# One sequence through all experts at once, the mixer and routing on a new timetable, and ScalarE in the mixer's norm

## The reference

```
x = x + 0.5 * ffn(layernorm(x))        # phase 1
x = x + mixer(layernorm(x))
x = x + 0.5 * ffn(layernorm(x))        # phase 2, same weights

ffn:   logits = tokens @ router_w.T    # 8 experts, top 2, softmax over the two
       each token: sum over its 2 experts of weight * (gelu(t @ w1[e]) @ w2[e])
       # w1[e] is 128x256, w2[e] is 256x128
mixer: v = x @ value_W.T; gates = sigmoid(x @ gate_W.T)   # 9 gates of 128
       out = sum over 9 shifts s of roll(v, -s) * gate_s   # shifts 0, +-1, +-4, +-16, +-32
       return layernorm(out) * gamma + beta
```

## Time and profile before

| | us |
|---|---|
| device time, median of 3 runs | 508.68 |
| lowest and highest of them | 504.05, 509.39 |
| device time of the profiled execution | 505.95 |
| its span, first to last instruction | 504.2 |
| TensorE busy with matmuls | 347.4 (69%) |
| VectorE busy | 286.4 (57%) |
| GpSimd busy | 254.5 (50%) |
| ScalarE busy | 181.6 (36%) |
| mean granted TensorE clock | 0.883 |

### The profile page before, as it was taken

One profiled execution on the slowest core, in us unless ns is written; L12 is line 12 of the kernel. 1 busy time (PEld: TensorE's weight loads), 2 busy tenths in 40 slices (PEclk: granted clock), 3 DMA queues, 4 the chain that ended last, 5 costly groups with the idle time before them and its releaser, 6 DMA issues.

```text
span 504.2 us, 8967 instructions
## 1 busy us (share of the span) xinstructions
PE 347.4 (69%) x2115; PEld 283.8 (56%) x2115; DVE 286.4 (57%) x1076; ACT 181.6 (36%) x422; POOL 254.5 (50%) x264
## 2 busy tenths in 40 slices
PE   1341885688899889996959977499753986288300
PEld 1330885587567756775537764277643975187300
DVE  6558054006666899889993699954997260020011
ACT  1010542343466456552425533355421342044100
POOL 0177717377767204767056173272664747570172
PEclk9999998798999999997779976889985798589955
DMA  8944447558527633453264242543447445845321
GB/s 253 297 142 137 148 136 225 158 157 254 178 88 203 190 106 89 121 157 115 69 183 121 86 150 90 155 111 101 145 150 215 135 142 166 245 128 155 101 73 47
DMA packets 102176, 74.66 MB, mean 148 GB/s; under 512 B 9704, under 2 KB 98032, under 8 KB 102128
## 3 DMA queue, kind: packets, MB, share of 16 engines
q1 hardware_dynamic: 93936, 57.30, 39.3%
q0 software_dynamic: 8192, 16.79, 11.2%
HBM read 48.50 MB, written 25.56 MB: 147 GB/s over the span
## 4 chain that ended last, share of the span: by engine, by line
PE 54%; DVE 15%; issue 12%; POOL 6%; DMA 5%; ACT 4%; SPq 2%; POOLq 0%; ACTq 0%; DVEq 0%
PE ps_u L341 16%; PE ps_u L402 14%; PE ps_d L353 14%; PE ps_t L331 5%; DMA xg<-xs 3%; PE ps_r L373 3%; DVE x_res L658 3%; POOL xs L759 3%; POOL g L771 3%; DVE prod L677 2%; DVE acc L680 2%; ACT y L476 2%; DVE stats L568 1%; DVE xn L588 1%; PE ps_t L395 1%
## 5 line engine op out<-in xcount | busy, mean ns | idle before, releaser
L771 POOL DMA_INDIRECT g<-ys,slot x128 | 127.2, 994 | 139.8 <-DMA ys<-y 86.1
L759 POOL DMA_INDIRECT xs<-xn,slot x128 | 126.3, 987 | 101.1 <-DVE slot L642 64.2
L341 PE MATMUL ps_u<-xT,w1s 128*128 128x128 f32 x736 | 114.7, 306 | 12.7 <-issue 9.9
L341 PEld LDWEIGHTS ps_u<-xT,w1s 128*128 128x128 f32 x736 | 106.0, 221 | 15.4 <-issue 11.6
L353 PE MATMUL ps_d<-w2s,hT 128*128 x736 | 105.3, 287 | 12.5 <-ACT y L476 11.4
L353 PEld LDWEIGHTS ps_d<-w2s,hT 128*128 128x128 f32 x736 | 95.1, 200 | 21.6 <-issue 21.6
L469 ACT ACTIVATE hT<-ps_u 128x512 f32<-128x512 f32 x96 | 55.6, 579 | 142.4 <-PE ps_d L353 126.8
L331 PE MATMUL ps_t<-ident,xg 128*128 128x128 f32 x184 | 43.5, 322 | 55.5 <-issue 48.8
L658 DVE SCALAR_TENSOR_TENSOR x_res<-g,wk,x_res 128x128 f32<-128x128 f32 x128 | 37.8, 348 | 75.3 <-DMA g<-ys,slot 74.0
L402 PE MATMUL ps_u<-xm,mixT 128*128 128x512 f32 x160 | 78.2, 622 | 0.4 <-ACT xm L453 0.4
L331 PEld LDWEIGHTS ps_t<-ident,xg 128*128 128x128 f32 x184 | 25.1, 162 | 75.2 <-issue 65.3
(11 more groups left out here) (79 smaller groups left out, 218.7 us busy)
## 6 DMA issues: line engine op xcount, KB each, us to landing
w1s<-in_L_ffn_w_dram SPq DMA_DIRECT2D x184, 128.0 KB
ys<-y SPq DMA_DIRECT2D x88, 128.0 KB, 2.1
xg<-xs SPq DMA_DIRECT2D x24, 384.0 KB, 4.4
xs<-zeros SPq DMA_DIRECT2D x10, 256.0 KB, 4.5
xg<-xs SPq DMA_DIRECT2D x8, 320.0 KB, 6.2
x_res<-in_L_attn_x_dram SPq DMA_DIRECT2D x4, 512.0 KB, 5.2
xs<-xn,slot POOLq DMA_INDIRECT x128
g<-ys,slot POOLq DMA_INDIRECT x128
```

What stands on the lines that cost most here:

```text
L341: i = pe.matmul(bank[:, c:c + P], w1s[:, G % NW, t, k * P:(k + 1) * P], xT[:, G % 2, t * P:(t + 1) * P], start=True, stop=True)
L759: pool.indirect_dma_start(out=xs[n % 2], out_offset=bass.IndirectOffsetOnAxis(ap=slot[:, n % RING, k, j:j + 1], axis=0), in_=xn[:, n % 2, ...
L771: pool.indirect_dma_start(out=g[:, k, j, :], out_offset=None, in_=ys[n % 2], in_offset=bass.IndirectOffsetOnAxis(ap=slot[:, n % RING, k, j ...
```

## The change

Four things change.

**Sequence 0, phase 1, is dense.** Segment 0 disappears. In its place a stage of 16 steps i (half of the tokens, expert e) takes 512 tokens through one expert: `dense_up` is two 128x512 products, `dense_gelu` two gelus, `dense_down` eight 128x128 products into the single bank `ps_d`, and `dense_add` four VectorE operations that add the result to x with each token's weight for this expert (`w_all`, zero where the expert isn't chosen). There is no scatter, no load of rows and no gather for it. All of w1 is loaded into `w1d` for it. `dense_down(i)` waits for `dense_add(i-1)`. Routing of segments 1, 2 and 3 (`ROUTER_IN`, `RANK_IN`) and the turns of the mixer's weights (`MIXW_IN`) are placed in these steps.

**Mixer and routing are placed anew.** Sequence 0's 20 units are at steps 3 to 9 of segment 1; those of the others stay where they were. Routing of segment 4 moves from segment 3 to segment 2 (router at step 5, rank at step 8); that of segment 7 is one step later than before. VectorE's order is written out.

**The row loads move.** Those of segments 5, 6 and 7 are at step 9 of the segment before, ahead of this step's w1 load and store; segment 4's is at step 2 of segment 3. The clearing of the scratch buffers and the loads of x are reordered at the start.

**The mixer's norm is shared.** `out_stats` also computes -mean/std (`shift`). ScalarE then computes z = o * rstd + shift in eight 128x128 operations (`normalise_mixed`, placed by `Z_AT` ahead of the last `copy_y` or of the next pairs). `out_add` adds beta, waits for z, multiplies by gamma and adds, in three 128x1024 operations instead of sixteen of 128x128 and one of 128x1024.

```diff
-    NG = NSEG * PAIRS
+    NG = (NSEG - 1) * PAIRS
+    NDENSE = 2 * E
...
-    TURN_STEP, TURN2_STEP = 8, 10
-    UNITS_FIRST = {10: 4, 11: 4}
-    UNITS_THEN = {0: 2, 1: 2, 2: 2, 3: 2, 4: 2, 5: 2}
-    GATES_FIRST, GATES_THEN = (1, 2), ((3, 4), (5,), (6, 7, 8, 9))
+    ROUTER_IN = {0: 1, 5: 2, 11: 3}
+    RANK_IN = {1: 1, 7: 2, 13: 3}
     MIXW_ROUNDS = (range(0, 4), range(4, 8), range(8, U))
-    MIXW_AT = {6: 0, 7: 1, 8: 2}
-
-
-    LOAD_STEP = (4, 2, 2)
-
-
-    def routed_in(n):
-        return n + 2 if n + 2 < BATCH else n + 1 if BATCH <= n + 1 < NSEG else None
-
-    def router_step(n):
-        return 3 if n + 2 < BATCH else 2
-
-    def rank_step(n):
-        return 5 if n + 2 < BATCH else 4
-
-
-    MOVES = [("to", 0), ("to", 1), ("to", 2), ("from", 0), ("to", 3), ("from", 1)]
-    for n in range(BATCH, NSEG):
+    MIXW_IN = {8: 0, 9: 1, 10: 2}
+    ROUTED = {2: (4, 5, 8), 4: (5, 2, 4), 5: (6, 2, 4), 6: (7, 3, 5)}
+    NORM2_AT = {(1, 3): 0, (2, 10): 1, (3, 10): 2, (4, 10): 3}
+    MIXED_AT = {(1, 11): 0, (3, 8): 1, (4, 8): 2, (5, 8): 3}
+    UNITS_AT = {0: {(1, 3): 2, (1, 4): 3, (1, 5): 3, (1, 6): 3, (1, 7): 3, (1, 8): 3, (1, 9): 3}}
+    for s in range(1, BATCH):
+        UNITS_AT[s] = {(s + 1, 10): 4, (s + 1, 11): 4, **{(s + 2, q): 2 for q in range(6)}}
+    Z_AT = {(2, 0): 0, (3, 11): 1, (4, 11): 2, (5, 10): 3}
+    LOAD_AT = {(2, 1): 3, (3, 2): 4, (4, 9): 5, (5, 9): 6, (6, 9): 7}
+    MOVES = [("to", 1), ("to", 2), ("to", 3), ("from", 1), ("to", 4), ("from", 2)]
+    for n in range(5, NSEG):
         MOVES += [("from", n - 2), ("to", n)]
     MOVES += [("from", NSEG - 2), ("from", NSEG - 1)]
...
     def units_at(n, q):
 
-        if 0 <= n - 2 < BATCH and q in UNITS_THEN:
-            before = sum(UNITS_FIRST.values()) + sum(c for k, c in UNITS_THEN.items() if k < q)
-            return n - 2, range(before, before + UNITS_THEN[q])
-        if 0 <= n - 1 < BATCH and q in UNITS_FIRST:
-            before = sum(c for k, c in UNITS_FIRST.items() if k < q)
-            return n - 1, range(before, before + UNITS_FIRST[q])
+        for s, at in UNITS_AT.items():
+            if (n, q) in at:
+                before = sum(c for k, c in at.items() if k < (n, q))
+                return s, range(before, before + at[n, q])
         return 0, range(0)
...
-            for b in range(2):
+            def load_x(b):
                 sp.dma_start(x_seq(b), x_tiles[:, b * TPS:(b + 1) * TPS, :]).then_inc(s_x[b], 16)
-                if b == 0:
-                    sp.dma_start(rt_raw[:], router_w).then_inc(s_rt, 16)
-            sp.wait_ge(s_zeros, 1)
-            clear(0)
+            load_x(0)
+            sp.dma_start(rt_raw[:], router_w).then_inc(s_rt, 16)
+            load_x(1)
+            sp.dma_start(w1d[:], w1.rearrange("e d f -> d e f")).then_inc(s_w1d, 16)
             for k in range(FH):
                 sp.dma_start(w2s[:, :, k * D:(k + 1) * D],
                              w2.rearrange("e (k p) d -> p k e d", p=P)[:, k, :, :]).then_inc(s_w, 16)
+            sp.wait_ge(s_zeros, 1)
             clear(1)
-            for b in range(2, BATCH):
-                sp.dma_start(x_seq(b), x_tiles[:, b * TPS:(b + 1) * TPS, :]).then_inc(s_x[b], 16)
+            load_x(2)
+            clear(0)
+            load_x(3)
...
             def load_rows(n):
-                sp.wait_ge(s_scat[n % 2], 16 * TOPK * TPS * (n // 2 + 1))
-                if n >= 2:
-                    sp.wait_ge(s_turned, turn_at["x", (n - 1) * PAIRS - 1] + 1)
+                sp.wait_ge(s_scat[n % 2], 16 * TOPK * TPS * (use_of(n) + 1))
+                if n >= 3:
+                    sp.wait_ge(s_turned, turn_at["x", pair_of(n - 2, PAIRS - 1)] + 1)
                 for c in range(CHUNKS):
                     w = slice(c * CT, min((c + 1) * CT, TILES))
                     sp.dma_start(xg[:, n % 2, w, :], xs_tiles[n % 2][:, w, :]).then_inc(s_xg[n % 2][c], 16)
 
...
             for G in range(NW):
                 load_w1(G)
-            load_rows(0)
-            for n in range(NSEG):
+            load_rows(1)
+            load_rows(2)
+            for n in range(1, NSEG):
                 for q in range(PAIRS):
-                    if n * PAIRS + q + NW < NG:
-                        load_w1(n * PAIRS + q + NW)
-                    if n + 1 < BATCH and q == LOAD_STEP[n]:
-                        load_rows(n + 1)
-                    store_y(n * PAIRS + q)
-                if BATCH <= n + 1 < NSEG:
-                    load_rows(n + 1)
+                    if (n, q) in LOAD_AT:
+                        load_rows(LOAD_AT[n, q])
+                    if pair_of(n, q) + NW < NG:
+                        load_w1(pair_of(n, q) + NW)
+                    store_y(pair_of(n, q))
                 if n - 1 >= BATCH:
                     store_out(n - 1)
             store_out(NSEG - 1)
...
             def router(n):
                 if n:
-                    pe.wait_ge(s_slot, n)
+                    pe.wait_ge(s_cnt, n)
+                src = xnT if n else xd
                 for k in range(2):
                     pe.wait_ge(s_tevac, turn_at["route", n, k] + 1)
                     for j in range(HT):
-                        i = pe.matmul(logits[:, k * HT + j, :], xnT[:, k, j * P:(j + 1) * P], rtT[:], start=True, stop=True)
+                        i = pe.matmul(logits[:, k * HT + j, :], src[:, k, j * P:(j + 1) * P], rtT[:], start=True, stop=True)
                 i.then_inc(s_lgt, 1)
 
             def rank(n):
                 pe.wait_ge(s_cnt, n + 1)
+                if n > 1:
+                    pe.wait_ge(s_slot, n - 1)
                 m = m_cnt[:].rearrange("p e j -> p (e j)")
...
+            def dense_up(i):
+                half, e = divmod(i, E)
+                if i == 0:
+                    pe.wait_ge(s_w1d, 16)
+                for k in range(FH):
+                    bank = product_bank(("dense", i, k))
+                    pe.matmul(bank, w1d[:, e, k * P:(k + 1) * P], xd[:, half, :], start=True, stop=True).then_inc(s_u, 1)
+            def dense_down(i):
+                half, e = divmod(i, E)
+                pe.wait_ge(s_uread, product_at["dense", i, FH - 1] + 1)
+                if i:
+                    pe.wait_ge(s_dread, i)
+                else:
+                    pe.wait_ge(s_w, 16 * FH)
+                for j in range(HT):
+                    for k in range(FH):
+                        t = pe.matmul(ps_d[:, j * D:(j + 1) * D], hd[:, i % 2, k, j * P:(j + 1) * P],
+                                      w2s[:, e, k * D:(k + 1) * D], start=(k == 0), stop=(k == FH - 1))
+                t.then_inc(s_dense, 1)
+            turn_norm(0)
+            router(0)
+            dense_up(0)
+            for i in range(NDENSE):
+                if i + 1 < NDENSE:
+                    dense_up(i + 1)
...
             def copy_mixed(s):
                 for k in range(2):
                     if s and k == 0:
-                        act.wait_ge(s_omix, s)
+                        act.wait_ge(s_z, s)
                     copy_turned(("mixed", s, k), o_mix[:, k * HT:(k + 1) * HT, :], bank_of(("mixed", s, k)))
+            def normalise_mixed(s):
+                act.wait_ge(s_shift, s + 1)
+                if s:
+                    act.wait_ge(s_omix, s)
+                for j in range(TPS):
+                    t = act.activation(z_mix[:, j, :], o_mix[:, j, :], ACT.Identity, scale=rstd[:, 2, j:j + 1],
+                                       bias=shift[:, 0, j:j + 1])
+                t.then_inc(s_z, 1)
...
             copy_turned(("router", 0), rtT[:], bank_of(("router", 0))[:, 0:E])
-            for n in range(2):
-                copy_norm(n)
-                gap_tanh(n)
-            for n in range(NSEG):
-                first = n * PAIRS
-                copy_rows(first)
-                copy_rows(first + 1)
-                gelu(first)
+            def dense_gelu(i):
+                for k in range(FH):
+                    n = product_at["dense", i, k]
+                    act.wait_ge(s_u, n + 1)
+                    if i >= 2 and k == 0:
+                        act.wait_ge(s_dense, i - 1)
+                    act.activation(hd[:, i % 2, k, :], ps_u[:, n % NU, :], ACT.Gelu).then_inc(s_uread, 1)
+            copy_norm(0)
+            dense_gelu(0)
+            gap_tanh(0)
+            for i in range(NDENSE):
+                if i + 1 < NDENSE:
+                    dense_gelu(i + 1)
+                if i in ROUTER_IN:
...
-                copy_y(first + PAIRS - 1)
+                    if n in ROUTED and q == ROUTED[n][2]:
+                        gap_tanh(ROUTED[n][0])
+                    if (n, q) in Z_AT:
+                        normalise_mixed(Z_AT[n, q])
+                copy_y(pair_of(n, PAIRS - 1))
...
+            def weigh_all():
+                by_e = [wk[:, 0, k, :].unsqueeze(1).broadcast_to([P, E, TPS]) for k in range(TOPK)]
+                dve.tensor_tensor(w_all[:, 0, :, :], chosen[:, 0, :, :], by_e[0], ALU.mult)
```

(105 more changed lines are left out.)

218 lines of the change are left out of this document (107 added, 111 removed).

## The result

The changed kernel takes 518.23 us (median of 4 runs, 515.66 to 521.86), the kernel before beside it 507.15 (4 runs, 504.05 to 509.39): ratio 1.0242, 95% interval 1.0183 to 1.0301. It is slower by 2.4%, where 502 us was forecast, 1.3% less than the 508.68 of the kernel before, with a range of 487 to 517. The profiled execution took 517.46 us with a span of 515.4, so the forecast span of 498.7 was missed by 16.7.

What follows compares the result with a forecast made beforehand. TensorE, VectorE's queue or late row loads behind GpSimd's scatter bound the stages. Terms of 107, 48.3, 55, 48.3, 63.1, 55.9, 53.8 and 67.3 gave a span of 498.7, 503 on the median's scale; forecast 502 us, range 487 to 517.

Steps and rivals of the forecast that it cites:

- The bound: Segments without routing are bound by TensorE (48.3 us), with routing by VectorE's queue (60.9); some start late, at 68.4.
- the dense stage: The stage replacing segment 0 ends at 107 us, with bounds of 101 and 121.
- segment 1: Segment 1 takes 48.3 us, like the present stage with 20 mixer units and no routing, ending at 155.3.
- two 3.9 us waits: In the dense stage TensorE idles about 4 us ahead of down(5) and again ahead of down(11), behind VectorE's norms.
- Rival 1: The dense stage stays at the lower clock and ends at 121 us, the whole at 516; chance 0.18.
- segment 2's term of 55: Segment 2, now with routing of sequence 4, takes 55 us, ending at 210.3; bounds 48.3 and 60.9.
- rival 2: Early load_rows holds SyncE, w1 loads come late, and 5 to 8 us of handover return elsewhere: 509 us; chance 0.20.
- Against: four w1 tiles are ahead: Argument against late w1 loads behind an early row load on SyncE: four w1 tiles are already ahead.
- segment 3's of 48.3: Segment 3, without the routing of sequence 4, again takes 48.3 us, ending at 258.6.
- norm(5), the next in its queue: Segment 4, VectorE: norm(5) starts no sooner than about 5 us in, now after 4; out_add's saving (5.6 to 3.7) counts nothing.
- segment 4's term: Segment 4 takes 63.1 us: 60.9 with rows loaded early, and 2.2 for ScalarE's eight normalise_mixed operations at the handover.
- The handovers: No gap before segments 4 and 5; GpSimd's scatter still binds the starts of 6 (+55.9 us) and 7 (+53.8).

Runs made afterwards that it cites:

- e14: e8 with the dense stage added and routing of segment 7 a step later; ratio 0.975 to the kernel before.
- e8: Kernel before with every row load at step 9 of the segment before, behind that step's w1 load; 490.35 us, ratio 0.9732.
- e3: Changed kernel with the mixer's norm wholly on VectorE again; ratio 1.0253 to the kernel before.
- e2: Changed kernel with w1 ahead of the row loads, and row loads of segments 3 and 4 at step 9 of the segment before; ratio 1.0017.
- e16: e10 with out_add of sequences 1 and 2 ahead of the next sequence's gates; ratio 0.9787 to the kernel before.
- e10: e2 with the mixer's normalisation back on VectorE alone; ratio 0.9966 to the kernel before.
- e13: Changed kernel with row loads of segments 5, 6 and 7 back behind the last store of the segment before; ratio 1.0421 to the kernel before.
- e4: Changed kernel with combine(1) and norm2(1) ahead of choose(4) and places(4) on VectorE in segment 2; ratio 1.0113 to the kernel before.
- e6: e2 with combine(1) and norm2(1) ahead of choose(4) and places(4) on VectorE in segment 2; ratio 1.0039 to the kernel before.
- e18: e16 with combine(1) and norm2(1) ahead of choose(4) and places(4) on VectorE in segment 2; ratio 0.9817 to the kernel before.
- e15: e8 with out_add of a sequence behind gates 1 and 2 of the next; ratio 0.9981 to the kernel before.

## Why the prediction was wrong

The measured 518.23 us lies above the range of 487 to 517, and no rival gave it.

**The bound, the dense stage, segment 1: right.** The adds, norms and their two 3.9 us waits came as followed; the add took 1.12 us, below the 1.2 taken. Rival 1 did not come: the granted clock is 0.92 over the stage, with the lower level only at places such as 81.50 (eight products, 16 records, in 3.76 us). The rule named beside it (the Trainium skill, TensorE: Matmul & The Clock Gate, HAM oscillation) is told there of a loop whose wait for its transfer is longer than its work in every round. Here only two of the sixteen adds held TensorE for 3.9 us, and no other for more than 1.31, so this run doesn't test it. The stage ends 9.5 us after the old segment 0, and in e14 segment 1 begins 13.3 us later than in e8 (104.49 against 91.23). That costs little in the end (e14 beside e8: 0.2%, inside the intervals): e14 is 4.3 us behind e8 at the last store of segment 1 and 2.8 at the end. I put this down to the routing of sequences 2 and 3, which the stage does and segments 0 and 1 had; no run tests it apart.

**The step that failed first: segment 2's term of 55, in which the row load ahead of w1 costs nothing; the reason is rival 2's "Against: four w1 tiles are ahead".** (The lead is four pairs, of up to two tiles each.) I asked what an early load_rows does to w1 only at step 9 of segments 4 to 6. The change also puts load_rows(3) at step 1 and load_rows(4) at step 2, ahead of that step's w1, and segment 2 was costed without its DMAs, though its text speaks of "the pairs that wait for w1 anyway". The row load's 1.5 MB use up that lead; that normalise_mixed(0) delays the y store ahead of it (162.53) adds little, since without it the wait is still 5.17 us (e3). Segment 2's term of 55 measured 64.2, segment 3's of 48.3 measured 51.9; e2 shows 2.2% for the pair, about 11 us. Rival 2 had the mechanism right, with 7 us and a chance of 0.20, but took it for the handovers' gain returning; that gain came, and this loss stands beside it. The row was at hand: the kernel before has a w1 wait of 5.0 us at 82.29 behind its own row load at step 4, which I passed over since it had no part in a term.

**The second: "norm(5), the next in its queue, starts no sooner than about 5 us into the segment where a norm now starts after 4; so I count the gain at nothing".** Its size was nearly right (275.57, 6.1 us into segment 4), but a delay on VectorE was set to zero without asking who waits for it. TensorE's turn at step 2 does, and the clock behind it. In the changed kernel one doesn't see this wait, since **ScalarE's operations**, the third step, hold TensorE for longer. I took 2.2 us for the eight; they take 3.18, and the estimate of 3.1 from the Trainium skill (ScalarE: Activation LUTs, What ACT_TABLE_LOAD costs) was the right one. The near row, a copy without pointer operands, was the wrong neighbour. TensorE waits 3.3 us at both handovers. That segment 4's term still came within 0.5 us is partly luck: the granted clock stayed at 1.00 behind this wait, and fell to 0.77 behind the same wait in segment 5 and to 0.76 in e2. Together order and operations cost 2.3% (e16 to e2), of which the order alone makes 1.8 (e10); my terms had 4.4 us for them, 0.9%.

**The handovers: right for segments 4 and 5, and the gain is real** (e8: 2.7% by loads alone, those of segments 1 to 3 among them; e13: 1.8% lost without those of 5 to 7). For 6 and 7 the forecast kept GpSimd as the bound, which held: 12.58 us before segment 7. GpSimd's timeline of the changed kernel, the first transfers of scatters 6 and 7:

```profile
364.50 1.00 POOL L911 DMA_INDIRECT xs<-xn,slot  x1 [4.87 <-DVE slot L720]
...
421.68 1.00 POOL L911 DMA_INDIRECT xs<-xn,slot  x1 [1.73 <-DVE slot L720]
```

From there to the first transpose 27.0 and 26.3 us pass, near the 26.4 taken. The 2.5 and 2.7 us beyond the terms are mostly in when the scatters start: 31.4 us into segment 5, not 29.5, behind the handover that held TensorE for 3.3 us and not 2.2, with the lower clock behind it; and 30.2 us into segment 6, not 27.4, behind a gather that ended 28.5 us in and not 27.3, and a wait of 1.62 us for w1 ahead of the routing. The 5.25 us wait of a down for ScalarE's copy at the end of segment 5 was rightly called hidden: it ends at 388.90, and TensorE then waits for the rows all the same.

**The sum.** Loads -2.7%, dense stage +0.2%, mixer and routing moved +0.4%, order and ScalarE +2.3%, early rows of 3 and 4 +2.2%: +2.4%. The differences add up by the way they are taken; the second and the third are inside the noise. The forecast had the gain and missed two losses of nearly its size. What stays open: why e4 gains 1.3% while the wait it removes is worth nothing in e6 and e18 was read from the waits, not tested by itself; and what ScalarE's operations cost with VectorE's old order.

## What to carry to other kernels

For each transfer that is moved, list what is queued behind it in its issuing queue in the next two steps, and count the bytes ahead of the small transfer that is due first; a load that is merely allowed to start early should start just early enough (e8, e2). An operation of little work that fills another queue's waiting time (out_add here) isn't free to move, and a part that saves nothing when removed alone may be one of two that hide each other: take out both before calling it free. Where a forecast sets a delay to zero, name who reads the result and in which fixed slot.

## What the runs showed of the hardware

A wait's length didn't say by itself what clock follows. After 1.66 us of waiting e15 ran two 128x512 products in 3.66 us (1.96 in e8), while after 3.31 us at 273.43 the changed kernel went on at a granted clock of 1.00 for 7 us, and e2 after the same 3.31 us at 261.06 showed 0.76 over the next 7 us. The two waits of 3.9 us in the dense stage were followed by 2.49 and by 3.76 us for the same eight products. VectorE's 128x128 add with one operand in PSUM costs no more than with all in SBUF (1.12 to 1.13 us for four, against 1.2 in the combine). A w1 tile of 128 KB landed 2.0 to 2.5 us after issue in segment 1, and 3.1 to 5.4 behind a row load of 1.5 MB in the same issuing queue.
